# The first four slot tiles of an expert layer gathered by TensorE products with one-hot matrices, instead of by a scatter to DRAM and a reload

## The reference

```python
x = hidden_states.reshape(-1, D)                  # 1024 normalised tokens, D = 128
gate_logits = x @ gate_weight.T                   # E = 16 experts
top_vals, top_idx = jax.lax.top_k(gate_logits, 2)
routing_w = jax.nn.softmax(top_vals, axis=-1)
mask = jnp.any(top_idx[:, :, None] == jnp.arange(E)[None, None, :], axis=1)
h = jax.nn.silu(jnp.einsum('td,efd->tef', x, w1)) # w1: (16, 512, 128)
h_sum = jnp.einsum('tef,te->ef', h, mask)         # per expert, over its tokens
y_mean = jnp.einsum('ef,edf->ed', h_sum / counts, w2)
out = jnp.einsum('tk,tkd->td', routing_w, y_mean[top_idx])
```

## Time and profile before

| | us |
|---|---|
| median of 3 runs | 277.55 (277.5 to 278.51) |
| the profiled execution | 276.65 |
| its span in the trace | 274.9 |
| PE busy | 224.9 (82%) |
| DVE busy | 206.9 (75%) |
| ACT busy | 175.7 (64%) |
| POOL busy | 48.1 (17%) |
| PE idle in front of the first transposes of slots (L1664) | 10.1 |

### The profile page before, as it was taken

How to read it: one execution, slowest core, us unless ns; L and a number is a source line. 1 busy time by engine, 2 the same in 40 slices (tenths; PEclk the granted TensorE clock), 3 DMA queues, 4 the chain that set the end, 5 groups by cost and what they waited for, 6 DMA issues and landing times.

```text
span 274.9 us, 7290 instructions
## 1 busy us (share of the span) xinstructions
PE 224.9 (82%) x2937; PEld 155.4 (57%) x2937; DVE 206.9 (75%) x480; ACT 175.7 (64%) x257; POOL 48.1 (17%) x64
## 2 busy tenths in 40 slices
PE   0799539999999998879999887988987505999984
PEld 0489416676766676656988765656656403233362
DVE  5675887999999999965326867788858957988312
ACT  5357897999999997049423547767566393665610
POOL 7003927910000000010000200000000577200000
PEclk9999957999999999997999999999999855899999
DMA  6930000000000000690000000000000015395002
GB/s 151 358 134 2 0 0 4 2 5 2 2 2 5 2 2 2 210 390 14 0 0 4 0 0 2 0 2 0 2 1 4 29 49 172 113 382 253 2 2 76
DMA packets 8558, 16.38 MB, mean 60 GB/s; under 512 B 720, under 2 KB 5072, under 8 KB 8272
## 3 DMA queue, kind: packets, MB, share of 16 engines
q1 hardware_dynamic: 8016, 14.90, 15.5%
q0 software_dynamic: 512, 1.05, 1.2%
HBM read 12.80 MB, written 3.15 MB: 58 GB/s over the span
## 4 chain that ended last, share of the span: by engine, by line
PE 52%; issue 16%; DVE 16%; ACT 7%; DMA 4%; POOL 2%; DVEq 1%; SPq 1%; ACTq 0%; POOLq 0%
PE ps L1681 8%; PE ps L1366 5%; DVE wide L987 5%; DVE t_k L1033 4%; PE ps L1472 3%; PE ps L1440 3%; DVE msda L992 3%; POOL slot_rows L510 2%; PE ps L1525 2%; PE ps L1704 2%; PE ps L1486 2%; DMA r_sb<-in_rows 2%; PE ps L1430 2%; PE ps L1498 2%; PE ps L1664 2%
## 5 line engine op out<-in xcount | busy, mean ns | idle before, releaser
L595 ACT ACTIVATE arena<-ps,one_less_sq 128x1024 bf16<-128x1024 f32 x64 | 67.3, 1113 | 4.9 <-PE ps L1352 4.9
L1366 PEld LDWEIGHTS ps<-arena 128*128 128x128 bf16 x1536 | 43.4, 97 | 20.0 <-issue 10.6
L1366 PE MATMUL ps<-arena 128*128 128x48 bf16 x1536 | 49.6, 184 | 5.1 <-DVE wide L987 4.6
L992 DVE TENSOR_REDUCE msda<-wide 128x768 f32 x32 | 46.1, 1513 | 0.0
L1352 PE MATMUL ps<-wide,sel 64*128 64x512 bf16 x128 | 25.9, 403 | 7.3 <-ACT arena L595 7.3
L987 DVE TENSOR_TENSOR wide<-ps,wide 128x768 f32<-128x768 f32 x32 | 30.1, 1009 | 1.4 <-PE ps L1366 1.4
L510 POOL DMA_INDIRECT slot_rows<-nrm,slots x16 | 16.1, 1005 | 66.2 <-ACT nrm L728 61.7
L1681 PE MATMUL ps<-arena,w_sb 128*32 x48 | 23.5, 635 | 0.0
L1033 DVE TENSOR_REDUCE t_k<-ps 128x2 f32<-128x512 f32 x32 | 20.5, 682 | 0.0
L664 ACT ACTIVATE wide<-ps 128x512 f32<-128x512 f32 x32 | 17.3, 594 | 1.4 <-PE ps L1510 1.3
L1689 PE MATMUL ps<-late,w_sb 128*32 128x512 f32 x80 | 16.6, 666 | 0.0
(11 more groups left out here) (320 smaller groups left out, 512.5 us busy)
## 6 DMA issues: line engine op xcount, KB each, us to landing
arena<-in_w_t SPq DMA_DIRECT2D x1, 4096.0 KB, 13.6
wide<-in_w_t SPq DMA_DIRECT2D x1, 4096.0 KB, 15.6
w_sb<-in_weights SPq DMA_DIRECT2D x1, 1544.0 KB, 8.8
slot_rows<-t_c SPq DMA_DIRECT2D x2, 768.0 KB, 10.3
late<-slot_rows SPq DMA_DIRECT2D x6, 256.0 KB, 3.3
x_sb<-in_x SPq DMA_DIRECT2D x4, 128.0 KB, 2.2
out<-xn SPq DMA_DIRECT2D x2, 256.0 KB, 2.2
r_sb<-in_rows SPq DMA_DIRECT2D x1, 288.0 KB, 4.8
```

Of the source, the lines that this page charges most:

```text
L595: nc.scalar.activation(hot[:, u, c:c + 5:4, :, :], ps[:, 2 * (c % 2):2 * (c % 2) + 2, :].rearrange("r p (b q) -> r p b q", b=B), ACT.Relu, ...
L992: nc.vector.tensor_reduce(msda[:, 4 * c + u:4 * c + u + 3:2, bass.ds(i, 1), :].rearrange("q b h d -> q b (h d)"), prod[:, c, :, :, :].rear ...
L1366: ins = nc.tensor.matmul(ps[:, 4 + b, p * NK * DH:(p + 1) * NK * DH], hot[:, u, p, b, :], rhs, start=(s == 0), stop=(s == PARTS - 1))
```

## The change

The constant `FIRST_STAGED` goes from 6 to 9, so ACT makes nine staged copies and DVE 63. DVE gets a new function `slot_rows`, which stands between `experts_of(0)` and `input_deviation(1)`. It builds `slot_hot`, for each of the four token tiles of half 0 a matrix of 128 tokens x 512 slots, which has a one where the slot is one of the token's two. For this POOL makes one row of numbers 0 to 511 (`slot_row`) early on. PE gets `bring_rows`, behind `project_out(1)` and in front of `rank(1)`: four products of `nrm` with `slot_hot`, accumulated in PSUM bank 3, which give the columns of slot tiles 0 to 3. SP no longer reloads group 0. All 16 scatters stay. On ACT eight staged copies, a wait, the ninth and `columns_out(0)` stand in front of `root(1)`, `columns_out(1)` goes into the loop, behind the four SiLUs of group 0, and `turn_slots(0)` is gone and `turn_slots(1)` stands behind `expert_tiles(0)`. SP's load of w2 also waits for `bring_rows`.

```diff
@@ -46,7 +46,7 @@
 HALF_GROUPS = HALF_TILES // GROUP
 SLOT_GROUPS = SLOT_TILES // GROUP
 STAGED = QUADS - 1
-FIRST_STAGED = 6
+FIRST_STAGED = 9
 ROUTE_AFTER = (2, 4)
 EPS = 1e-5
 ROUND = 1.5 * 2 ** 23
@@ -231,6 +231,7 @@
 
         ff_flat = wide[:, 0:GE * T]
         v_cols = ff_flat[:, 0:TILES * AH * VGRAIN].rearrange("k (t h c) -> k t h c", t=TILES, h=AH)
+        slot_hot = ff_flat[:, 0:4 * GROUP * P].rearrange("q (t s) -> q t s", t=4)
         nmax = t0_k[:, :, :].rearrange("q t c -> q (t c)").rearrange("q (t n c) -> q t n c", t=2, n=PAIRS)
 
         prob_t = [shared[:, UH * 2 * HW:].rearrange("k (i c) -> k i c", i=UH),
@@ -254,6 +255,8 @@
         slot_of = sb("slot_of", [P, 4, E])
         picked_slot = sb("picked_slot", [P, TOPK, 4, E])
         slots = sb("slots", [P, TOPK, TILES], I32)
+        slots_f = sb("slots_f", [P, TOPK, 4])
+        slot_row = sb("slot_row", [P, GROUP * P])
         ended = sb("ended", [P, HALF_TILES, E])
         expert_of = sb("expert_of", [P, 2, HALF_TILES])
         expert_at = sb("expert_at", [P, 2, HALF_TILES], I32)
@@ -291,9 +294,9 @@
 
         ld_x = [sem(f"ld_x{b}") for b in range(B)]
         ld_v, ld_r, ld_wa, ld_wb, ld_wc, ld_w1, ld_w2 = sems("ld_v ld_r ld_wa ld_wb ld_wc ld_w1 ld_w2")
-        zeros_ready, rows_zeroed, late_consts = sems("zeros_ready rows_zeroed late_consts")
+        zeros_ready, rows_zeroed, slot_hot_ready = sems("zeros_ready rows_zeroed slot_hot_ready")
         scattered = sems("scattered0 scattered1")
-        reloaded = [sem(f"reloaded{g}") for g in range(SLOT_GROUPS)]
+        reloaded = [None] + [sem(f"reloaded{g}") for g in range(1, SLOT_GROUPS)]
         stored, pool_step, dve_step, consts, sel_ready, dve_consts = sems(
             "stored pool_step dve_step consts sel_ready dve_consts")
         ident_ready, ramp_ready, sel_low_ready = sems("ident_ready ramp_ready sel_low_ready")
@@ -383,7 +386,7 @@
 
 
 
-        NMAX_ZEROED, V_ZEROED, ROUTE_ZEROED = 1, 2, 3
+        NMAX_ZEROED, V_ZEROED, ROUTE_ZEROED, SLOTS_COUNTED = 1, 2, 3, 4
         HOT_CREDIT, G_CREDIT, FREE_CREDIT = 2, 3, 2
         CONSTS = 6
         VALUE_ORDER = (2, 3, 0, 1)
@@ -411,15 +414,16 @@
             sp.dma_start(w1_sb, w1_t.rearrange("e d f -> d e f")).then_inc(ld_w1, 16)
 
             sp.wait_ge(st_mm, UH * UNITS)
-            for g in range(SLOT_GROUPS):
+            for g in range(1, SLOT_GROUPS):
                 h, n = g // HALF_GROUPS, g % HALF_GROUPS
-                if n == 0:
+                if g in (1, HALF_GROUPS):
                     sp.wait_ge(scattered[h], 16 * 4 * TOPK)
                 sp.dma_start(x_slots[:, GROUP * g:GROUP * g + GROUP, :],
                              scratch[h].rearrange("(n s) c -> s n c", s=P)[:, GROUP * n:GROUP * n + GROUP, :]).then_inc(
                     reloaded[g], 16)
             sp.wait_ge(pv_mm, UNITS)
             sp.wait_ge(x2_ready, 2)
+            sp.wait_ge(cols_mm, GROUP)
             sp.dma_start(w2_sb, w2_t).then_inc(ld_w2, 16)
             for h in range(2):
                 sp.wait_ge(y_out_ready, h + 1)
@@ -459,7 +463,7 @@
             nc.gpsimd.iota(quad_i[:, :, :, :], pattern=[[1, QUADS], [0, E // QUADS], [-1, QUADS]], base=0,
                            channel_multiplier=0)
             nc.gpsimd.affine_select(out=tok_before[:, :], in_=one_c[:, 0:1].to_broadcast([P, P]), compare_op=ALU.is_ge,
-                                    fill=0.0, base=-1, pattern=[[1, P]], channel_multiplier=-1).then_inc(late_consts, 1)
+                                    fill=0.0, base=-1, pattern=[[1, P]], channel_multiplier=-1)
 
             def hat(out, at, k, spare, n, ready):
                 nc.gpsimd.tensor_scalar(out, at, 1.0 - k, 1.0, ALU.add, ALU.min)
@@ -499,6 +503,8 @@
             nc.gpsimd.memset(v_cols[:, :, :, AD + 1:], 0.0)
             nc.gpsimd.memset(v_cols[:, :, :, AD:AD + 1], 1.0).then_inc(zeroed, 1)
             nc.gpsimd.memset(route[:, :, :], 0.0).then_inc(zeroed, 1)
+            nc.gpsimd.iota(slot_row[:, :], pattern=[[1, GROUP * P]], base=0, channel_multiplier=0,
+                           allow_small_or_imprecise_dtypes=True).then_inc(zeroed, 1)
 
             pool.wait_ge(rows_zeroed, 32)
             for t in range(TILES):
@@ -755,31 +761,33 @@
                     nc.scalar.activation(staged_at[n], w1_sb[:, bass.ds(at[n % STAGED][n // STAGED], 1), :].rearrange(
                         "d e f -> d (e f)"), ACT.Copy).then_inc(staged_first, 1)
 
-            stage_first(range(0, 2))
+            def columns_out(g):
+                act.wait_ge(cols_mm, GROUP * g + GROUP)
+                nc.scalar.activation(x_cols[:, GROUP * P * g:GROUP * P * (g + 1)], ps[:, 3, :] if g == 0 else slots_bank(g),
+                                     ACT.Copy).then_inc(cols_ready, 1)
+
+            stage_first(range(0, 8))
+            act.wait_ge(ap_mm, TILES)
+            stage_first(range(8, FIRST_STAGED))
+            columns_out(0)
             root(1)
             normalise(1)
             x2_out(0)
             x2_out(1)
-            stage_first(range(2, FIRST_STAGED))
 
             act.wait_ge(gap_ready, 1)
             nc.scalar.activation(e2[:, :], gap[:, :], ACT.Exp).then_inc(e2_ready, 1)
 
             nc.scalar.activation(table_junk[:, :], eps_c[:, :], ACT.Silu)
 
-            def columns_out(g):
-                act.wait_ge(cols_mm, GROUP * g + GROUP)
-                nc.scalar.activation(x_cols[:, GROUP * P * g:GROUP * P * (g + 1)], slots_bank(g),
-                                     ACT.Copy).then_inc(cols_ready, 1)
-
-            columns_out(0)
-            columns_out(1)
             for g in range(SLOT_GROUPS):
                 for t in range(GROUP * g, GROUP * g + GROUP):
                     act.wait_ge(h_mm, t + 1)
                     if t >= len(hidden_at):
                         act.wait_ge(sum_mm, (t - len(hidden_at)) // GROUP + 1)
                     nc.scalar.activation(hidden_at[t % len(hidden_at)], ps[:, 2 + t % 4, :], ACT.Silu).then_inc(h_ready, 1)
+                if g == 0:
+                    columns_out(1)
                 if g + 2 < SLOT_GROUPS:
                     columns_out(g + 2)
                 if g in ROUTE_AFTER:
@@ -1186,9 +1194,24 @@
                     nc.vector.tensor_copy(staged_at[n % len(staged_at)], w1_sb[:, bass.ds(at[q][t % GROUP], 1), :].rearrange(
                         "d e f -> d (e f)")).then_inc(staged, 1)
 
+            def slot_rows():
+
+                dve.wait_ge(slots_ready, 1)
+                dve.wait_ge(zeroed, SLOTS_COUNTED)
+                dve.wait_ge(pv_mm, UNITS)
+                link(nc.vector.tensor_copy(slots_f[:, :, :], slots[:, :, 0:4]))
+                for t in range(4):
+                    ins = nc.vector.tensor_scalar(slot_hot[:, t, :], slot_row[:, :], slots_f[:, 0, t:t + 1], None, ALU.is_equal)
+                link(ins)
+                for t in range(4):
+                    nc.vector.scalar_tensor_tensor(out=slot_hot[:, t, :], in0=slot_row[:, :], scalar=slots_f[:, 1, t:t + 1],
+                                                   in1=slot_hot[:, t, :], op0=ALU.is_equal,
+                                                   op1=ALU.add).then_inc(slot_hot_ready, 1)
+
             scale(0)
             place(0)
             experts_of(0)
+            slot_rows()
             input_deviation(1)
             rank_logits(1)
             choose(1)
@@ -1651,6 +1674,17 @@
             turn_outputs(1)
             output_logits(1)
             project_out(1)
+
+            def bring_rows():
+
+                pe.wait_ge(prob_ready, UH * UNITS)
+                for t in range(4):
+                    pe.wait_ge(lnf["norm"], t + 1)
+                    pe.wait_ge(slot_hot_ready, t + 1)
+                    ins = nc.tensor.matmul(ps[:, 3, :], nrm[:, t, :], slot_hot[:, t, :], start=(t == 0), stop=(t == 3))
+                ins.then_inc(cols_mm, GROUP)
+
+            bring_rows()
             rank(1)
             turn_x2(0)
             turn_x2(1)
@@ -1715,10 +1749,10 @@
                     nc.tensor.transpose(ps[:, 7, P * (t % 4):P * (t % 4) + P], route[:, t, :], ident[:, :]).then_inc(rt_mm, 1)
 
             pe.wait_ge(x2_c_ready, 2)
-            turn_slots(0)
-            turn_slots(1)
             for g in range(SLOT_GROUPS):
                 expert_tiles(g)
+                if g == 0:
+                    turn_slots(1)
                 if g in ROUTE_AFTER:
                     turn_route(ROUTE_AFTER.index(g))
                 if g + 2 < SLOT_GROUPS:
```

## The result

The changed kernel took 281.35 us (median of 6 runs, 280.18 to 282.06). The kernel before took 278.45 us beside it (6 runs, 277.5 to 280.22). The ratio is 1.0103 (95% interval 1.0069 to 1.0138), so the change costs 2.9 us. The direction was forecast, the size was not: +1.65 us was expected, and the time lies 0.15 us above the range. The profiled execution took 282.06 us, with a span of 280.3 us where the earlier trace rows belong to a span of 274.9.

What follows compares the result with a forecast made beforehand. PE's gapless 22 us, started by group 3's reload, was taken as the bound. The reload 1.9 us late, less 1.05 spare, plus 0.1 gave +0.95; with part of the clock lost, +1.65 on 277.55: 279.2 us, range 276.8 to 281.2.

Steps and rivals of the forecast that it cites:

- What bounds: PE's gapless 22.00 us from 241 to 263; only what moves its start, set by group 3's reload, moves the end.
- What would show it: Signs: first expert tile near 227.3, scatter 9 near 227, group 3's reload at about 241.9, clock 0.50 between 236 and 243.
- D: DVE's added time for slot_rows: 4.6 us, ends 4.2 and 6.0; as rival: gain kept, 273.4 us, chance 0.03.
- Rival F: On DVE, compares held by POOL's scatters, 1.48 instead of 0.41 each: D = 8.9 us, time 283.5 us; chance 0.04.
- Scatters and reload: POOL's ninth scatter starts at 227.1 instead of 225.48; group 3's reload is 1.9 us late, landing at 241.85: +0.95 us.
- Group 1's tiles at 237.2: PE's expert_tiles(1) waits for DVE's staged copies, there at 237.2, and ends at about 241.1 if its clock is full.
- The clock: PE's clock may fall in the wait before 237.2: +2.4 us instead of +0.95; the middle, +1.65, was taken.
- The reference: Differences were taken on one profiled execution of 276.65 us, 0.9 less than the median, and added to the median 277.55.
- B: Rival: PE's clock holds and only the scatters count, +0.95 us, 278.5 us; chance 0.27.
- C: Rival: not slower, as POOL's ninth scatter is delayed within the 1.05 us to spare, or not at all (276.6); chance 0.10.
- E: Rival: bring_rows at half clock costs 0.6 us and the clock its full 1.45: 280.6 us, 282 at worst; chance 0.14.

Runs made afterwards that it cites:

- the second trace of the same kernel: The kernel before, traced again with no edit: one run, 278.98 us, span 277.2.
- the run with 14 and 12 products: The changed kernel with 14 and 12 products of constants in PE's waits in front of groups 0 and 1: 281.02 us, ratio 1.0112.
- the changed kernel's second trace: The changed kernel run again with no edit: 280.89 us against 277.63 for the kernel before, ratio 1.0121.

## Why the prediction was right or wrong

*What bounds.* Right in its main point: only the start of the 22 us behind group 3's transposes counts, and group 0's early start (forecast for 227.3, measured 228.46) is given back. The gain in front was not worth anything in any run. "What would show it" named PE idle in front of group 3's transposes; it was not, as group 1 was late instead.

*D.* Forecast 4.6, measured 4.83 (214.90, where `input_deviation(1)` would have stood 0.2 us later in this trace, to 219.73). The compares took 1.90 together, with a pitch of about 0.47 instead of 0.43, and the four others 2.74. Rival F falls: the four compares took 0.47 to 0.67 us each beside the scatters, with a median of 0.50. The rule that the two engines exclude each other for the whole instruction (the Trainium skill, SBUF — State Buffer, "Who interferes with whom") is not borne out in that form. On DVE's side 0.2 us were lost on one compare, and on POOL's side two scatters beside `slot_rows` took 1.14 and 1.15 where most take 0.96, as single ones did in the trace of before as well.

*Scatters and reload.* Right. Scatter 9 was forecast for 227.1 and came at 227.43, and the reload landed at 241.8 (forecast 241.85).

*Group 1's tiles at 237.2.* **This step failed.** The prediction took DVE's copies as the last to come in front of group 1, and group 3's reload (241.85) as the last in front of group 3. Both were on time (the copies at 236.29, forecast 236.1), but group 1's columns hang on ACT behind the fourth SiLU, and ACT saw PE's fourth tile 5 us late. The tiles began at 240.09, and group 3 was turned at 246.37, 4.5 us behind its reload. I had taken such a signal as immediate, because in the trace of before the SiLUs follow their tiles. There they also do so beside scatters, which the second trace of the same kernel does not repeat. By its orders the changed kernel exposes itself more: `columns_out(1)` waits for PE's tiles and for transposes behind them, where before it waited only for transposes that were through before the first tile. Where the signals came at once (the changed kernel without the last scatters), DVE's copies were the last to come, as forecast. A `columns_out(1)` in front of the SiLUs was not tried; the run with 14 and 12 products shows that the transposes' own signal can be as late.

*The clock.* The mechanism was right, the term mis-sized. I took 0.7 us, half of the price for a fall in the wait before group 1. The wait was 5.3 us instead of 2 to 4, and the clock fell in it or right behind it: group 1 took 6.3 us here and 5.1 in the second trace, against 3.6 at full clock. That is 1.5 to 2.7 us. In the first pair of traces the sum closes: group 1 began 2.65 us later than in the earlier trace rows (240.09 for 237.44) and took 2.7 us longer, which makes the 5.4 us. Holding the clock gives back 0.8 to 1.0%, most of the loss, though ACT's signals stay late.

*The reference.* The sum was made on differences to one execution (span 274.9) whose like did not come back in two further traces of that code (277.2, and 276.2 with the row of numbers). The traced execution (276.65 us) is also faster than each of the 69 runs of that code that the other kernels are compared with (276.79 us and up). Against the second trace the start of the long stretch moves from 243.33 to 246.37, by 3.0 us. That this is close to the 2.9 measured is partly luck of the pair: with the changed kernel's second trace (244.79) it is 1.5 us.

*The rivals.* B, C and D did not come. E gave the right size, 280.6 to 282, and not its mechanism: `bring_rows` did run partly at half clock (5.37 us for four products) and ended at 223.3, a little behind the forecast's 221 to 223, but `columns_out(0)` ended at 224.0 and `root(1)` followed at 224.10, when its variance was ready.

*What stays open.* Why PE's finished work reaches ACT late. The runs show that the delay goes with the scatters (held back, it moves with them; left out, it is gone), and that DVE can be hit too: in the second trace of the kernel before it waited 2.04 us for the same signal. The semaphore events in the trace files, which no view above prints, put the lateness on PE's side. In the first trace of the changed kernel PE's increment for the fourth tile is recorded at 238.85, and those for the transposes, which had run from 233.7 to 234.8, follow it from 238.88 to 239.12, 0.03 us apart. As the ends of matmuls are modelled, this does not tell whether the results or only their signals were late. Nor are scatters under way the whole condition: the first trace of the kernel before had them and no delay, and with the row of numbers alone the SiLUs came at 237.90, 1.5 us behind the last landing of a scatter on record (236.40). Every run here was made with the profiler's recording, so whether the delay would be there without it was not tried.

## What to carry to other kernels

Before work is moved ahead, ask which later stretch has no gap, and what alone sets its start. Here 3 us were gained ahead of it and it began later. A signal that one trace shows as immediate may not be so in the next execution: take a second trace of the same kernel before a sum rests on it, and count the signals from the busy engine that a copy others need (group 1's columns) stands behind. That fewer of them would have helped here was not tried. Where PE must wait before a dense stretch, look at the clock with which it starts.

## What the runs showed of the hardware

**Signals of PE were late beside indirect DMAs.** In the second trace of the kernel before, ACT started four SiLUs from 237.22 on whose tiles had ended from 232.4 on. In the first trace it started none late. In the changed kernel ACT stood idle for 3.75 us in front of one in the first trace and for 5.08 us in the second. In the two traces without the last eight scatters the SiLUs of group 0 followed their tiles.

**One scatter took twice its time in two versions.** In the two versions with `slot_rows` behind the gap instruction the ninth scatter stands beside three copies of DVE that follow at once. The timeline of POOL in the first of them:

```profile
223.65 1.15 POOL L516 DMA_INDIRECT slot_rows<-nrm,slots  x1 [0.30 <-issue]
225.10 2.02 POOL L516 DMA_INDIRECT slot_rows<-nrm,slots  x1 [0.30 <-issue]
227.43 0.96 POOL L516 DMA_INDIRECT slot_rows<-nrm,slots  x1 [0.30 <-issue]
```

It took 2.02 us there and 2.03 in the other, where a scatter takes 0.96. That the copies did it is not shown: in the trace of before six such copies ran from 223.24 to 225.40, and the scatter of 224.10 in their midst took 1.08.
